# Three orders inside the queries' step: TensorE's output, VectorE's floor and finish, ScalarE's squares

## The chip, the core and the metric

The kernel runs on one core of one Trainium2 chip. The metric is the device time of one execution in microseconds (us). The engines work in parallel, each through its own instructions in order, and meet at semaphores: TensorE (PE, with its weight loads PEld), VectorE (DVE), ScalarE (ACT), GpSimd (POOL), and SyncE (SP), which here issues the transfers between HBM and SBUF.

## What is computed

Two layers with residuals on x of 16 x 256 x 64 x 64 (float32). Layer 0 is a group norm and a 3 x 3 convolution whose kernels are rotated per image by a small network. Layer 1 is a group norm and a focused linear attention with 8 heads and a 5 x 5 depthwise convolution of V.

```
x = x + conv(_gn(x))                      # layer 0: rotated 3x3 kernels, modulated
xt = _gn(x) as tokens                     # 4096 tokens of 256 channels
q = (relu(xt @ Wq.T + bq) + 1e-06) / scale
k = (relu(xt @ Wk.T + bk) + 1e-06) / scale
v = xt @ Wv.T + bv
q = q**3 / norm(q**3) * norm(q)           # the same for k
kv_state = einsum('bjc,bjd->bcd', k, v)
z = 1.0 / (einsum('bic,bc->bi', q, k.sum(axis=1)) + 1e-06)
out = einsum('bic,bcd->bid', q, kv_state) * z[..., None]
out = out + depthwise5x5(v)
x = x + out @ Wproj.T + bproj
```

## The kernel before, in words

Every engine has its own program, written by hand; the order of the code is the order of its instructions, and semaphore counters join them. The 16 images (batches b) go through three phases each: keys and values (16 half units of 256 tokens), the depthwise convolution, and the queries. Beside the queries of image b the engines do the layer 0 convolution of image b+2 and the input of the attention of image b+1. So batches 0 to 13 carry a convolution in the queries' phase, batch 14 only the next input, and batch 15 neither. Batches 0 to 12 are a hardware loop, the last three are unrolled.

The queries' phase is a software pipeline of steps (u, p), numbered n = 2u + p, of which each moves half a unit (256 tokens). In step n:

- TensorE (`step_q`, L1615) makes attention of half n-2, the output of half n-4, the transposes of O of half n-3, the projection of half n, the transposes of Q of half n-1, and a half plane of the convolution. In the step of u = 8 the keys of the next batch stand in the projection's place, in that of u = 9 its values.
- VectorE (`step_q`, L1066) does conv_out, cube of half n-1, denominators, inverses and quotients of half n-2, finish of half n-4 (it adds the output to the residual), result_stats, the cast of the attention's input (from u = 3), high (p = 1 only: the memsets of the borders of plane u+1 and its cast), ratio of half n-1, low_out of half n-3, and floor_max of half n, which waits for the projection.
- ScalarE (`step_q`, L1352) does planes (p = 1: the norm of plane u+1), sixths of half n-1 (behind cube), the norm of the attention's input, high_out of half n-3, shift (p = 0, behind result_stats), transposed_q (the copy QT of the transposes of Q, half n-1), norms (behind ratio), and squares of half n (behind floor_max).
- SyncE (`step`, L438) loads in p = 0 the residual of unit u-1 and stores x1. In p = 1 it loads the pixels, then waits until finish of both halves of unit u-2 is done (L375) and stores them, then loads the attention's input U (from u = 3), and then, when GpSimd has made the low half of plane u+1, the plane u+2 into PL (for u up to 5). All of it is one queue in order. PL is one buffer; ScalarE takes plane u+2 at the head of step (u+1, 1).

Attention of half n-2 in step n waits for the copy QT made in step n-1. Cube of half n waits for its squares. The output waits for low_out of its half.

Of the kernel before, what the change touches and what calls it, by code (L numbers as in the profile page):

```python
# [5 lines left out]
def conv_then_focused_attention(  # L6
# [58 lines left out]
    with ctx:  # L65
# [637 lines left out]
        def _(dve):  # L703
# [255 lines left out]
            def result_stats(c, k):  # L959
                g, q = divmod(k, 2)  # L960
                dve.wait_ge(x1_rdy, 2 * GROUPS * c + k + 1 + X1_CR)
                v.bn_stats(ST[:, 1, g, q, :], pixel_tile(c, g)[:, UNIT * q:UNIT * (q + 1)]).then_inc(s1_rdy, 1)
# [8 lines left out]
            def floor_max(n, p):  # L971
                dve.wait_ge(f_full, n + 1)
                fl = FL[:, :].unsqueeze(1).broadcast_to([P, 2, C])
                f = F[p][:, :].rearrange("p (t n) -> p t n", t=2)
                v.tensor_tensor(f, f, fl, ALU.max).then_inc(f_max, 1)  # L975
# [75 lines left out]
            def finish(b, u, p):  # L1051

                m = b * PAIRS + 2 * u + p
                dve.wait_ge(y_full, m + 1)
                dve.wait_ge(r_in[u % 2], Y_OUT * (b * NU // 2 + u // 2 + 1))
                r = R[:, u % 2, :, :, 2 * HD * p:2 * HD * (p + 1)].rearrange("p h m n -> p (h m) n")
                v.scalar_tensor_tensor(r, PP[:, :].rearrange("p (a n) -> p a n", n=2 * HD), out_fac, r,  # L1057
                                       ALU.mult, ALU.add).then_inc(y_rdy, 1)
# [8 lines left out]
            def step_q(b, u, p, live, nxt, keys, keys_end, conv):  # L1067
                n = b * 2 * PAIRS + PAIRS + 2 * u + p
                k = 2 * u + p - 1
                if conv and 0 <= k < 2 * GROUPS:  # L1070
                    conv_out(b + 2, k)
                if live(p - 1) or keys and p == 1 or keys_end and p == 0:
                    cube(n - 1, 1 - p)
                if live(p - 2):
                    denominators(b, u - 1, p)
                    inverses(b, u - 1, p)
                    quotients(b, u - 1, p)
                if live(p - 4):
                    finish(b, u - 2, p)
                if conv and 0 <= k < 2 * GROUPS:  # L1080
                    result_stats(b + 2, k)
                if nxt:
                    attn_input(b + 1, u - 3, p, False)
                if conv and p == 1 and u + 1 < GROUPS:
                    high(b + 2, u + 1)
                if live(p - 1):
                    ratio(n - 1, 1 - p, S6, S2)
                elif keys and p == 1:
                    ratio(n - 1, 1 - p, S2, S6)
                if live(p - 3):  # L1090
                    low_out(b, u - 2 + p, 1 - p)
                if live(p) or keys:
                    floor_max(n, p)
                if keys_end and p == 0:
                    scale_k(n - 2, 0)

# [148 lines left out]
        def _(act):  # L1245
# [43 lines left out]
            def squares(n, p):  # L1289
                act.wait_ge(f_max, n + 1 + MAX_CR)  # L1290
                act.wait_ge(f_cube, n + 1)
                act.wait_ge(f_six, 2 * n + 2)
                for t in range(2):
                    ts = slice(t * C, (t + 1) * C)
                    a.activation(K2[:, p, ts], F[p][:, ts], ACT.Square, scale=inv_a,  # L1295
                                 accum_out=S2[:, 2 * p + t:2 * p + t + 1]).then_inc(f_sq, 1)
# [57 lines left out]
            def step_q(b, u, p, live, nxt, keys, keys_end, conv):  # L1354
                n = b * 2 * PAIRS + PAIRS + 2 * u + p
                if conv and p == 1 and u + 1 < GROUPS:
                    planes(b + 2, u + 1)
                if live(p - 1) or keys and p == 1 or keys_end and p == 0:
                    sixths(n - 1, 1 - p)
                if nxt:  # L1360
                    attn_input(b + 1, u - 3, p)
                if live(p - 3):
                    high_out(b, u - 2 + p, 1 - p)
                if conv and p == 0 and 1 <= u <= GROUPS:
                    shift(b + 2, u - 1)
                if live(p - 1):
                    transposed_q(b, u - 1 + p, 1 - p)
                    norms(n - 1, 1 - p, den_eps)
                elif keys and p == 1:
                    norms(n - 1, 1 - p, inv_a2)  # L1370
                if live(p) or keys:
                    squares(n, p)

            def shift(c, g):

                act.wait_ge(s1_rdy, 2 * (GROUPS * c + g) + 2)
                tile = pixel_tile(c, g)
                a.activation(tile, tile, ACT.Identity, bias=BPC[:, g:g + 1]).then_inc(shifted, 1)
# [77 lines left out]
        def _(pe):  # L1456
# [143 lines left out]
            def output(b, u, p):  # L1600
                m = b * PAIRS + 2 * u + p
                pe.wait_ge(ol_rdy, m + 1 + OL_CR)
                pe.wait_ge(y_rdy, m + Y_CR)
                for h in range(HALVES):
                    k = 0
                    for kk in range(HALVES):
                        for wa, xa in PASSES:
                            ins = t_.matmul(PP[:, h * C:(h + 1) * C], WP[:, wa, kk, h * P:(h + 1) * P],  # L1608
                                            OT[:, xa, kk, 2 * P * p:2 * P * (p + 1)].rearrange(
                                                "p (y m x) -> p m y x", y=2, m=4),  # L1610
                                            start=(k == 0), stop=(k == 5))
                            k += 1
                ins.then_inc(y_full, 1)

            def step_q(b, u, p, live, conv, nxt):  # L1615

                if live(p - 2):
                    attention(b, u - 1, p)
                if live(p - 4):
                    output(b, u - 2, p)  # L1620
                if live(p - 3):
                    transpose_o(b, u - 2 + p, 1 - p)
                if live(p):
                    pe.wait_ge(f_cube, b * 2 * PAIRS + PAIRS + 2 * u + p + 1)
                    project(b, u, p, F, 0)
                elif nxt and u == NU:
                    keys(b + 1, 0, p)
                if live(p - 1):
                    transpose_q(b, u - 1 + p, 1 - p)
                if conv and u < GROUPS:  # L1630
                    convolve(b + 2, u, p)
                if nxt and u == NU + 1:
                    if p == 0:
                        pe.wait_ge(o_rdy, 2 * PAIRS * (b + 1) + O_CR)
                        carry(pe)
                    values(b + 1, 0, p)
# [147 lines left out]
```

## Time and profile before

| | us |
|---|---|
| median of 3 runs (3966.69 to 3974.39) | 3972.8 |
| the profiled execution | 3968.21 |
| its span | 3966.1 |
| TensorE busy | 3555.9 (90%) |
| VectorE busy | 2978.9 (75%) |
| ScalarE busy | 2704.6 (68%) |
| GpSimd busy | 1425.3 (36%) |
| L1057 finish, L975 floor_max: median of one | 0.742, 0.690 |
| L1346 copy of QT: median of one | 0.567 |

The middle of batch 5 is used as the sample. Its attention (L1587) starts at 1573.45 in step 2, 1579.11 in 3, 1585.18 in 4, 1592.46 in 5, 1599.74 in 6, 1607.02 in 7, 1614.31 in 8, 1621.59 in 9, 1628.87 in 10, 1636.37 in 11, 1643.76 in 12, 1651.40 in 13, 1658.79 in 14, 1666.45 in 15, 1673.84 in 16 and 1679.65 in 17. The other batches of the loop repeat this within some 0.03 us a step.

A share of busy time is an average over phases with different limits; what a change in the queries' step is worth is read from the steps themselves: who waits there, and for whom. A row of a timeline gives the start, the duration, the engine, the line, the operation, what it writes and reads, and in brackets the idle time before it with what ended it.

### The profile page before, as it was taken

What the parts mean: (1) busy time and instruction counts of PE and PEld (TensorE: products, weight loads), DVE (VectorE), ACT (ScalarE), POOL (GpSimd) and SP (SyncE); (2) the same over time, 40 slices, a digit from 0 to 9 for tenths busy, and PEclk for the clock granted to TensorE, in tenths of its full rate; (3) what the DMA queues carried; (4) which work ended last, traced back from release to release, by engine and by line L of the source; (5) the groups of instructions that cost most, each with busy time, mean ns of one, the idle gap of its engine ahead of it and who ended that gap; (6) DMA issues with size and microseconds to landing.
All of it is one profiled execution on the core that took longest, in us unless ns stands there. A gap on an engine that the chain in (4) does not pass through costs nothing.

```text
span 3966.1 us, 96093 instructions
## 1 busy us (share of the span) xinstructions
PE 3555.9 (90%) x27980; PEld 2859.5 (72%) x27980; DVE 2978.9 (75%) x8235; ACT 2704.6 (68%) x7348; POOL 1425.3 (36%) x1318
## 2 busy tenths in 40 slices
PE   0569989999999999999999998999999899999797
PEld 0138777777877777777777877777787777778686
DVE  6766877868778786877868687786868778585756
ACT  2247776776777677677766767776677767677675
POOL 4532442514334252433525243351424425140302
PEclk9989999999999999999999999999999999999999
DMA  4672634536354452635436263443636344260302
GB/s 156 202 236 65 173 98 143 161 90 186 109 155 116 131 173 82 184 112 149 130 111 192 71 184 113 138 141 108 179 91 178 99 145 132 79 181 22 102 17 75
DMA packets 560047, 516.42 MB, mean 130 GB/s; under 512 B 97600, under 2 KB 491968, under 8 KB 559552
## 3 DMA queue, kind: packets, MB, share of 16 engines
q1 hardware_dynamic: 555200, 508.99, 43.4%
q8 instruction: 220, 3.60, 0.4%
q14 instruction: 275, 2.25, 0.2%
q10 hardware_dynamic: 4352, 1.57, 0.2%
HBM read 351.06 MB, written 134.22 MB: 122 GB/s over the span
## 4 chain that ended last, share of the span: by engine, by line
PE 34%; DVE 29%; issue 17%; ACT 14%; DVEq 2%; DMA 1%; ACTq 1%; SPq 1%; POOL 1%; POOLq 0%
PE F L1557 7%; ACT K L1295 6%; PE VAB L1557 6%; PE F L1518 6%; PE VAB L1518 5%; PE T L1529 4%; DVE F L975 3%; DVE XR L1064 3%; ACT K L1301 3%; DVE XR L1057 3%; DVE XHL L969 3%; DVE K L981 2%; DVE XR L1046 2%; DVE RATIO L989 2%; PE PP L1608 2%
## 5 line engine op out<-in xcount | busy, mean ns | idle before, releaser
L1518 PE MATMUL F<-WQ,XHL 128*128 128x256 f16 x6144 | 819.3, 274 | 27.7 <-ACT V L1335 19.1
L650 POOL TENSOR_TENSOR XR<-XR,V 128x512 f32<-128x512 f32 x256 | 325.6, 1272 | 1042.9 <-DVE XR L1046 1042.9
L1518 PEld LDWEIGHTS F<-WQ,XHL 128*128 128x128 f16 (+1 forms) x6144 | 602.2, 99 | 106.8 <-issue 33.9
L1301 ACT ACTIVATE K<-K,SCAL 128x256 f32<-128x256 f32 x1024 | 512.4, 505 | 209.2 <-DVE K L981 208.2
L634 POOL TENSOR_TENSOR SL<-PL,SL 128x1122 f16<-128x1122 f32 x112 | 259.7, 2319 | 1065.2 <-DVE SL L947 1065.2
L1504 PE MATMUL SM<-SL,BD 128*128 128x512 f16 x2688 | 634.9, 385 | 0.0
L1295 ACT ACTIVATE K<-F,SCAL 128x256 f32<-128x256 f32 x1024 | 473.4, 469 | 232.0 <-DVE F L975 231.6
L975 DVE TENSOR_TENSOR F<-F,FL 128x512 f32<-128x512 f32 x512 | 354.1, 692 | 176.7 <-PE F L1520 175.4
L981 DVE TENSOR_TENSOR K<-K,F 128x512 f32<-128x512 f32 x512 | 349.3, 682 | 167.2 <-ACT K L1295 166.6
L1504 PEld LDWEIGHTS SM<-SL,BD 128*128 128x128 f16 x2688 | 261.0, 97 | 284.1
L1608 PE MATMUL PP<-XR,WP 128*128 128x256 f16 x3072 | 385.6, 276 | 67.8 <-DVE XR L1064 67.8
L1518 PE MATMUL VAB<-WQ,XHL 128*128 128x256 f16 x3072 | 414.6, 277 | 0.0
L1608 PEld LDWEIGHTS PP<-XR,WP 128*128 128x128 f16 x3072 | 297.9, 99 | 114.7 <-DVE XR L1064 76.9
L641 POOL TENSOR_TENSOR XHL<-U,XHL 128x512 f16<-128x512 f32 x256 | 297.9, 1170 | 208.8 <-DVE XHL L969 208.8
L1529 PE MATMUL T<-VT,K 128*128 128x129 f32 x2048 | 292.4, 287 | 71.7 <-DVE K L996 62.7
L1587 PEld LDWEIGHTS VAB<-KVS,VT 128*128 128x128 f32 x2048 | 261.6, 190 | 110.5 <-issue 46.7
L1518 PEld LDWEIGHTS VAB<-WQ,XHL 128*128 (+1 forms) x3072 | 305.5, 99 | 37.4
L1529 PEld LDWEIGHTS T<-VT,K 128*128 128x128 f32 x2048 | 258.0, 197 | 102.0 <-DVE K L996 94.3
L1587 PE MATMUL VAB<-KVS,VT 128*128 128x132 f32 x2048 | 282.4, 281 | 48.5 <-ACT VT L1346 44.1
L1557 PE MATMUL F<-V,TP 128*128 128x248 f16 (+1 forms) x2304 | 289.1, 282 | 0.0
L1520 PE MATMUL F<-BQ,ONES 128*128 128x256 f16 x1024 | 281.1, 275 | 0.0
L1307 ACT ACTIVATE NORM<-RATIO,SCAL 128x2 f32<-128x2 f32 x512 | 151.9, 297 | 175.8 <-DVE RATIO L989 175.1
(194 smaller groups left out, 6948.0 us busy)
## 6 DMA issues: line engine op xcount, KB each, us to landing
XR<-xr SPq DMA_DIRECT2D x132, 512.0 KB, 5.2
U<-x SPq DMA_DIRECT2D x256, 256.0 KB, 3.8
XR<-x SPq DMA_DIRECT2D x256, 256.0 KB, 4.1
out<-XR SPq DMA_DIRECT2D x256, 256.0 KB, 3.8
PL<-xp SPq DMA_DIRECT2D x112, 561.0 KB, 3.8
RX<-xr SPq DMA_DIRECT2D x118, 512.0 KB, 4.2
x<-RX SPq DMA_DIRECT2D x448, 128.0 KB, 2.1
BD<-RX SPq DMA_DIRECT2D x240, 96.0 KB, 2.2
```

What stands on the lines that cost most here:

```text
L641: g_.tensor_tensor(lo, U[:, u % 2, h].rearrange("p m y x -> p y m x"), hi, ALU.subtract).then_inc(l_rdy, 1)
L650: g_.tensor_tensor(o, o, fm, ALU.add).then_inc(o_rdy, 2)
L975: v.tensor_tensor(f, f, fl, ALU.max).then_inc(f_max, 1)
L981: v.tensor_tensor(K3[:, p, :], K2[:, p, :], F[p][:, :], ALU.mult).then_inc(f_cube, 1)
L1295: a.activation(K2[:, p, ts], F[p][:, ts], ACT.Square, scale=inv_a, accum_out=S2[:, 2 * p + t:2 * p + t + 1]).then_inc(f_sq, 1)
L1301: a.activation(K2[:, p, t * C:(t + 1) * C], K3[:, p, t * C:(t + 1) * C], ACT.Square, scale=inv_a, accum_out=S6[:, 2 * p + t:2 * p + t + 1] ...
L1504: ins = t_.matmul(conv_bank(c, q)[:, :], BD[:, j, HALVES * wa + h, sx, P * sy:P * (sy + 1)], half[:, xa, 16 * q + sy:16 * q + sy + 16, sx: ...
L1518: t_.matmul(o, XHL[:, xa, h, at], WQ[:, wa, h, c0:c0 + C], start=(k == 0), stop=False)
L1529: ins = t_.matmul(T[h][:, 0:P + 1], K3[:, p, t * C + h * P:t * C + (h + 1) * P], VT[:, p, t, h, 0:P + 1], start=False, stop=False)
L1557: ins = t_.matmul(bank[:, lo:hi], TP[:, c, d, ta, :], V[:, c, va, lo + sh:hi + sh], start=(k == 0), stop=(k == 8))
L1587: ins = t_.matmul(VA[t][:, h * KVC:(h + 1) * KVC], QT[:, p, h, t * P:(t + 1) * P], KVS[:, h, :], start=True, stop=True)
L1608: ins = t_.matmul(PP[:, h * C:(h + 1) * C], WP[:, wa, kk, h * P:(h + 1) * P], OT[:, xa, kk, 2 * P * p:2 * P * (p + 1)].rearrange("p (y m x ...
```

## The change

In the queries' step

- TensorE makes the output behind the projection (or the next batch's keys), no longer between attention and the transposes of O;
- VectorE does floor_max right behind result_stats, and finish last;
- ScalarE does the squares ahead of the copy QT and of norms, no longer behind them.

No instruction of the computation is added or removed, and SyncE's and GpSimd's programs are as they were.

```
@@ VectorE, step_q @@
-                if live(p - 4):
-                    finish(b, u - 2, p)
                 if conv and 0 <= k < 2 * GROUPS:
                     result_stats(b + 2, k)
+                if live(p) or keys:
+                    floor_max(n, p)
                 if nxt:
                     attn_input(b + 1, u - 3, p, False)
...
                 if live(p - 3):
                     low_out(b, u - 2 + p, 1 - p)
-                if live(p) or keys:
-                    floor_max(n, p)
+                if live(p - 4):
+                    finish(b, u - 2, p)
@@ ScalarE, step_q @@
+                if live(p) or keys:
+                    squares(n, p)
                 if live(p - 1):
                     transposed_q(b, u - 1 + p, 1 - p)
                     norms(n - 1, 1 - p, den_eps)
                 elif keys and p == 1:
                     norms(n - 1, 1 - p, inv_a2)
-                if live(p) or keys:
-                    squares(n, p)
@@ TensorE, step_q @@
                 if live(p - 2):
                     attention(b, u - 1, p)
-                if live(p - 4):
-                    output(b, u - 2, p)
                 if live(p - 3):
                     transpose_o(b, u - 2 + p, 1 - p)
                 if live(p):
...
                     keys(b + 1, 0, p)
+                if live(p - 4):
+                    output(b, u - 2, p)
```

VectorE, a step with the attention's input, p = 0 (L1046 quotients, L1057 finish, L962 result_stats, L975 floor_max, L969 cast of the input, L1064 low_out, L956 conv_out):

```order
 L1046 TENSOR_TENSOR XR<-VAB,Z 128x2x32x4 x2
-L1057 SCALAR_TENSOR_TENSOR XR<-PP,SCAL,XR 128x8x64
 L961 REGISTER_ALU
 L962 BN_STATS ST<-RX 128x6
+L972 REGISTER_ALU
+L975 TENSOR_TENSOR F<-F,FL 128x512
 L967 ISA
 L969 CAST XHL<-U 128x512
```

Floor_max went ahead of the cast, and finish left its place behind the quotients.

ScalarE, a step of p = 0 (L1378 shift, L1346 copy QT, L1307 norms, L1295 squares):

```order
 L1378 ACTIVATE RX<-RX,BPC 128x1024
-L1346 COPY VT<-T 128x512
-L1306 REGISTER_ALU
-L1307 ACTIVATE NORM<-RATIO,SCAL 128x2
-L1290 REGISTER_ALU
-L1292 REGISTER_ALU
-L1295 ACTIVATE K,S<-F,SCAL 128x256 x2
+L1290 REGISTER_ALU
+L1292 ISA
+L1295 ACTIVATE K,S<-F,SCAL 128x256 x2
+L1346 COPY VT<-T 128x512
+L1307 ACTIVATE NORM<-RATIO,SCAL 128x2
```

The squares moved between shift and the copy QT.

TensorE, a step from number 4 on (L1608 output, L1596 transposes of O, L1518 and L1520 projection):

```order
-L1608 MATMUL PP<-XR,WP 128x256 x12
-L1596 MATMUL T<-MATS,XR 128x128 x4
-L1518 MATMUL F<-WQ,XHL 128x256 x6
-L1520 MATMUL F<-BQ,ONES 128x256
-L1518 MATMUL F<-WQ,XHL 128x256 x6
-L1520 MATMUL F<-BQ,ONES 128x256
+L1596 MATMUL T<-MATS,XR 128x128 x4
+L1518 MATMUL F<-WQ,XHL 128x256 x6
+L1520 MATMUL F<-BQ,ONES 128x256
+L1518 MATMUL F<-WQ,XHL 128x256 x6
+L1520 MATMUL F<-BQ,ONES 128x256
+L1608 MATMUL PP<-XR,WP 128x256 x12
```

The output moved behind the projection, next to the transposes of Q.

## Rows read from the trace of the kernel before

**Rows 1.** Timeline of TensorE, batch 5, steps 11 to 13.

```profile
1636.37 1.16 PE L1587 MATMUL VAB<-KVS,VT 128*128 128x132 f32 x8
1637.37 1.47 PE L1608 MATMUL PP<-XR,WP 128*128 128x256 f16 x12
...
1639.12 0.82 PE L1518 MATMUL F<-WQ,XHL 128*128 128x256 f16 x6
...
1641.08 2.84 PE L1504 MATMUL SM<-SL,BD 128*128 128x512 f16 x12
1643.76 1.06 PE L1587 MATMUL VAB<-KVS,VT 128*128 128x132 f32 x8
...
1651.40 1.16 PE L1587 MATMUL VAB<-KVS,VT 128*128 128x132 f32 x8
```

**Rows 2.** Timeline of ScalarE, the same stretch: shift, QT, planes, sixths, input, squares.

```profile
1634.62 1.15 ACT L1378 ACTIVATE RX<-RX,BPC 128x1024 f32<-128x1024 f32 x1
1635.68 0.56 ACT L1346 COPY VT<-T 128x512 f32<-128x512 f32 x1
...
1637.79 1.32 ACT L1281 ACTIVATE PL<-PL,PR 128x1122 f32<-128x1122 f32 x1
1639.00 0.50 ACT L1301 ACTIVATE K<-K,SCAL 128x256 f32<-128x256 f32 x1
...
1639.98 0.81 ACT L1286 ACTIVATE U<-U,PR 128x512 f32<-128x512 f32 x1
...
1645.37 0.47 ACT L1295 ACTIVATE K<-F,SCAL 128x256 f32<-128x256 f32 x1 [1.05 <-DVE F L975]
```

**Rows 3.** Timeline of VectorE, the same: input's cast, plane's cast, low_out, floor, cube.

```profile
1641.05 0.56 DVE L969 CAST XHL<-U 128x512 f16<-128x512 f32 x1
...
1642.52 1.03 DVE L947 CAST SL<-PL 128x1122 f16<-128x1122 f32 x1
...
1643.91 0.74 DVE L1064 SCALAR_TENSOR_TENSOR XR<-T,SCAL,XR 128x512 f16<-128x512 f32 x1
1644.57 0.69 DVE L975 TENSOR_TENSOR F<-F,FL 128x512 f32<-128x512 f32 x1
...
1646.51 0.69 DVE L981 TENSOR_TENSOR K<-K,F 128x512 f32<-128x512 f32 x1 [0.61 <-ACT K L1295]
```

**Rows 4.** Timeline of batch 14: two starts of attention, a cast, a cube.

```profile
3702.83 0.96 DVE L969 CAST XHL<-U 128x512 f16<-128x512 f32 x1
...
3703.82 1.17 PE L1587 MATMUL VAB<-KVS,VT 128*128 128x132 f32 x8 [1.36 <-ACT VT L1346]
...
3706.58 0.69 DVE L981 TENSOR_TENSOR K<-K,F 128x512 f32<-128x512 f32 x1 [1.09 <-ACT K L1295]
...
3710.19 1.17 PE L1587 MATMUL VAB<-KVS,VT 128*128 128x132 f32 x8 [1.36 <-ACT VT L1346]
```

**Rows 5.** Timeline of TensorE, batch 15: an attention, and the last output.

```profile
3886.76 1.17 PE L1587 MATMUL VAB<-KVS,VT 128*128 128x132 f32 x8 [0.68 <-ACT VT L1346]
...
3959.99 1.48 PE L1608 MATMUL PP<-XR,WP 128*128 128x256 f16 x12 [1.57 <-DVE XR L1064]
```

**Rows 6.** Timeline of TensorE, batch 5: its last two outputs.

```profile
1686.33 1.48 PE L1608 MATMUL PP<-XR,WP 128*128 128x256 f16 x12 [2.24 <-DVE XR L1064]
...
1692.07 1.48 PE L1608 MATMUL PP<-XR,WP 128*128 128x256 f16 x12 [2.29 <-DVE XR L1064]
```

**Rows 7.** Timeline of SyncE's queue, batch 5: store, U load, PL load.

```profile
1641.99 1.44 SPq L378 DMA_DIRECT2D out<-XR  x2
1643.77 1.66 SPq L348 DMA_DIRECT2D U<-x  x2
1646.28 0.38 SPq L328 DMA_DIRECT2D PL<-xp  x1
```

**Rows 8.** DMA issues, time to landing: the PL load of 1646.28, and that of 1600.91.

```profile
PL<-xp SPq DMA_DIRECT2D x1, 561.0 KB, 5.1
...
PL<-xp SPq DMA_DIRECT2D x1, 561.0 KB, 3.7
```

More of the change, by code:

```diff
@@ L1077, in step_q @@
                     quotients(b, u - 1, p)
-                if live(p - 4):
-                    finish(b, u - 2, p)
                 if conv and 0 <= k < 2 * GROUPS:
                     result_stats(b + 2, k)
+                if live(p) or keys:
+                    floor_max(n, p)
                 if nxt:
@@ L1091, in step_q @@
                     low_out(b, u - 2 + p, 1 - p)
-                if live(p) or keys:
-                    floor_max(n, p)
+                if live(p - 4):
+                    finish(b, u - 2, p)
                 if keys_end and p == 0:
@@ L1365, in step_q @@
                     shift(b + 2, u - 1)
+                if live(p) or keys:
+                    squares(n, p)
                 if live(p - 1):
@@ L1370, in step_q @@
                     norms(n - 1, 1 - p, inv_a2)
-                if live(p) or keys:
-                    squares(n, p)
             def shift(c, g):
@@ L1618, in step_q @@
                     attention(b, u - 1, p)
-                if live(p - 4):
-                    output(b, u - 2, p)
                 if live(p - 3):
@@ L1627, in step_q @@
                     keys(b + 1, 0, p)
+                if live(p - 4):
+                    output(b, u - 2, p)
                 if live(p - 1):
```

## The prediction, made before the changed kernel ran

> **What bounds the kernel now.** First the busy shares on the first page of the profile: TensorE is busy for 90% of the span, VectorE 75%, ScalarE 68%, so a step counts only where TensorE stands still in it, or is made to. So the second view is TensorE's timeline of the queries' steps, with the starts of attention as a ruler (numbers of steps: 2u+p). Three kinds of batches differ.
>
> Batches 0 to 13 carry a convolution in steps 0 to 15. In one late step attention takes 1.00 us, output with O's transposes 1.75, projection with Q's transposes 1.96, the convolution 2.68: 7.39, of which 0.1 belongs to the wait before it; the next step ends 7.64 later [rows 1]. Without waits a step is 7.28, as steps 4 to 9 are. From step 4 to step 16 attention moves from 1585.18 to 1673.84: 88.66, against 12 x 7.28 = 87.36. So 1.3 us per batch are waits, all in the last six steps. Their source is on VectorE: floor at 1644.57, the squares on ScalarE 0.80 later, and cube not before 1646.51, after an idle 0.61 [rows 2, 3]. Two late steps take 15.03 [rows 1]; less two such waits VectorE's own work is 13.8 of the 14.56 that TensorE needs, and with them it is over.
>
> Batch 14 has no convolution: its steps take 6.37, VectorE idles 1.09 in each before cube, and TensorE 1.36 before attention [rows 4]. Batch 15 has less VectorE work: 5.55 a step, which is TensorE's own 4.7 (1.00 + 1.75 + 1.96 [rows 1]) plus the time until the copy of QT, for which it idles 0.68 [rows 5].
>
> Third, the end of each batch. There output waits 2.24 and then 2.29 us for low_out [rows 6]; at the very end 1.57 [rows 5].
>
> **The change, part by part.** Nothing is added; the orders of TensorE, VectorE and ScalarE change, SyncE's does not.
>
> Floor ahead, finish last. Floor(n) moves ahead of cast, ratio and low_out, right after the sums. The squares then run under these and cube(n) no longer waits. This takes the 0.61 and 1.09 off VectorE. In batches 0 to 13 TensorE gets at most the 1.3 us. In batch 14 VectorE's load falls from 6.37 to 5.3, below the 5.55 that TensorE and the QT copy need in batch 15: 0.82 less for each of 9 steps, 0.3 for the one before, 7.7 in all.
>
> Output behind the projection. This brings floor's input 1.3 us earlier, else floor would wait in its new place. For TensorE the sum stays. At a batch's end O's last transposes no longer stand behind an output that waits. I walked it with the rows' durations: seen from attention of step 16 the last output starts 16.7 later instead of 18.23 (1692.07 [rows 6] less 1673.84), a gain of 1.55. In batch 14 I get 1.5, because the copies of V then wait for the U load of unit 7; at the end of batch 15, 1.9.
>
> Squares ahead of QT's copy. They put 0.92 us (two of 0.47 [rows 2]) in front of a copy that TensorE's next attention needs. Where the convolution stands between, it has 2.68 us of cover, but in steps of p=0 shift stands in front too: shift 1.06, copy to attention 0.69 [rows 1, 2], and squares between. The cover is gone at step 2, where shift is late: attention of step 3 comes 0.35 later. At step 16, without a convolution, it comes 0.8 later (inside the 1.55). In steps 2 to 4 of batches 14 and 15 neither output nor convolution is there, and projection, floor, squares, copy become one chain: attention is later by 0.95, 0.95 and 0.8 to 1.2, so 2.7 in batch 14 and 3.2 in batch 15.
>
> The queue behind finish. This speaks against the change. SyncE is in order: it waits for finish of step n, issues the two stores, then the U load, then the plane load PL, which ScalarE needs at the head of step n+2 (n odd). Today finish comes early and the store is held by a pixel load; PL is held by GpSimd's low half (the U load is out at 1645.43, PL starts 1646.28 [rows 7]). Now finish is VectorE's last work in the step that also has the plane's memsets and cast, and PL has one buffer. The cycle, from the start of planes on ScalarE: sixths +1.21, attention's input +0.98 [rows 2], its cast +0.90, the plane's cast +1.47, low_out +1.39, finish +0.66 [rows 3] (finish is taken to start where floor did), its end and the store +0.84, U +1.78 [rows 7], PL +1.97 (the U issues 1.66, and a gap of 0.3), then its landing L and 0.1 for the wait: 11.3 + L, less 0.2 where the U issue is shorter. L was 3.7 for a PL load without U in front and 5.1 and more with it [rows 8]. In between, L = 4.1, is what I take, since the pixel load, just ahead of the store in those late cases, is then some four us ahead and done. So a pair takes 15.2 to 15.3, and three pairs per batch are behind a U load (planes 5, 6, 7: steps 9 to 15). Against 3 x 14.56 that is +2.2, with 0.05 for step 8. Ends: with L = 3.7, +1.0; with 5.1, +5.2 per batch.
>
> The port. The cast of the attention's input takes 0.56 [rows 3], and in batch 14, beside a GpSimd addition, 0.96 [rows 4]. In its new place, by my walk, it starts some 0.3 before GpSimd's addition ends. If it ran at half speed beside it, that would cost 0.15 a step, and the sum has room for that in VectorE's idle time. The Trainium skill (SBUF — State Buffer, section SBUF: two separate sides) says that of the two engines the one that starts first holds their shared port pair for its whole instruction, and the other is blocked. By it the cast would be held for those 0.3, and the sum would be the same, except at steps where VectorE is late, which would be later by 0.15 more.
>
> **Sum**, on the profiled execution (span 3966.1, time 3968.2). Batches 0 to 12: +0.35 + 2.25 - 1.3 - 1.55 = -0.25 each, -3.2. Batch 13, whose code is unrolled, has only 0.5 of waits to give back: 0.35 + 2.0 - 0.5 - 1.55 = +0.3. Batch 14: +2.7 - 7.7 - 1.5 = -6.5. Batch 15: +3.2 - 1.9 = +1.3. In all -8.1. The profiled execution lies 4.6 under the median 3972.8, so I forecast 3972.8 - 8 = 3965.
>
> **Rivals.**
> - The plane load does not bind. If L is 3.4 or less, or the chain has slack that I missed, pairs take 14.6: -2.4 per batch against the sum's -0.25. Times 14 this is -30 more: 3935. For it: PL loads of 3.7 exist [rows 8]. Against it: U and store go just ahead. The Trainium skill (DMA: Bandwidth & Descriptors, section Anatomy of one DMA — SWDGE (gpsimd) path) fits one transfer by 2.0 us plus its bytes over 436 GB/s, for another way of issuing. For 561 KB this is an estimate of 3.3 us, and by it this rival would hold; the trace disagrees, with 3.7 and 5.1 [rows 8].
> - Slower: the queue behind finish binds fully. One mechanism, one place: PL lands late and holds ScalarE's planes, with everything behind them. Each us of L costs 3 us per batch, 42 in all. It decides from L = 4.3 (total zero). With L = 5.1, as today's late ones, +42 on the forecast: 4007; with L = 6, 4045. For it: U directly before PL, as in today's late cases. Against it: the pixel load is gone from in front.
> - No change: the change does what it says, but TensorE has its own 7.28 nearly everywhere, and what the ends give the heads and copies take. Mine is the sum of small terms of both signs, so 3972 is near.
> - The squares' place costs more than priced. In a p=0 step cube, sixths, attention's input, O's high copy, shift, squares and QT's copy follow each other: attention of the next step is 6.33 after VectorE's first instruction of the step. That fits into 7.28 if VectorE starts less than 0.95 late, and each 0.2 more costs 5 steps x 14 x 0.2 = 14 us: 3980.
>
> **How the numbers follow.** A measurement of this kernel tells about 0.2%, 8 us, from no change. I give my forecast 0.38, the free plane load 0.20, the bound queue 0.20, no change 0.12, the copies 0.10. The forecast lies on the border of 0.2%, so its chance is halved over faster and same, with little over slower. Faster 0.45, same 0.28, slower 0.27. The range is to leave out 1 in 5: it reaches 3930 (free plane load with a little more) and 4010 (L = 5.1).
>
> **What would show it.** Right: in batches 0 to 12, cube without idle time before it; steps 4 to 9 at 7.28; pairs 9-11, 11-13, 13-15 of 15.0 to 15.5, with ScalarE's planes released by the DMA of PL; attention of step 3 later by 0.35; idle before the last outputs 1.2 instead of 2.3; batch 14 at 5.55 a step after a head 2.7 longer; batch 15 with att(1) and att(2) later and the same 5.55. Wrong: pairs of 14.6 (then the queue was overpriced), pairs over 16, or ScalarE's copy releasing attention in the middle steps.

## The result: 1.4% slower, and the profile after

| | before | after |
|---|---|---|
| median (3 runs; 4 runs) | 3972.8 | 4026.45 (4024.36 to 4031.19) |
| after over before, 95% interval | | 1.0138 [1.0125, 1.0151] |
| profiled execution, its span | 3968.21, 3966.1 | 4024.36, 4022.3 |
| TensorE busy | 3555.9 (90%) | 3576.2 (89%) |
| VectorE busy | 2978.9 (75%) | 2946.3 (73%) |

The forecast was 3965, in a range of 3930 to 4010. The time is 61 us above the forecast and 16 above the range's upper end. A fourth run of the kernel before, beside the changed one, took 3967.30.

The spans of the profiled executions added up by stage, from TensorE's timeline (us; a loop batch is the mean of batches 1 to 12; "attention 2" is the one of step 2):

| stage | loop batch before, after | batch 13 | batch 14 | batch 15 |
|---|---|---|---|---|
| keys and values | 65.74, 66.57 | 65.70, 63.98 | 61.07, 61.07 | 61.37, 61.99 |
| to attention 2 | 44.48, 44.52 | 42.43, 42.52 | 39.93, 40.83 | 39.30, 40.96 |
| attention 2 to 17 | 106.22, 111.46 | 105.01, 110.07 | 88.62, 87.67 | 80.54, 82.59 |
| attention 17 to the next batch | 17.62, 15.82 | 14.81, 13.47 | 16.01, 13.47 | |

So the loss stands in one place: 5.2 us per batch between attention 2 and 17. In batch 5 attention now starts, from step 9 on, 7.98, 8.28, 7.38, 8.01, 8.36 and 8.27 us apart, where it was 7.28 to 7.67 before; steps 4 to 9 stay at 7.28. Over the loop, the three pairs from step 9 to step 15 take 16.34 on average, against the 15.25 of the forecast and TensorE's 14.56.

Who is waited for there is on ScalarE. Timeline of ScalarE after, batch 5, steps 13 and 15: planes, and between them sixths, squares and the copy of QT.

```profile
1660.73 1.32 ACT L1281 ACTIVATE PL<-PL,PR 128x1122 f32<-128x1122 f32 x1 [1.96 <-DMA PL<-xp]
...
1669.18 0.51 ACT L1301 ACTIVATE K<-K,SCAL 128x256 f32<-128x256 f32 x1 [2.27 <-DVE K L981]
...
1672.49 0.46 ACT L1295 ACTIVATE K<-F,SCAL 128x256 f32<-128x256 f32 x1
...
1673.39 0.57 ACT L1346 COPY VT<-T 128x512 f32<-128x512 f32 x1
...
1677.37 1.32 ACT L1281 ACTIVATE PL<-PL,PR 128x1122 f32<-128x1122 f32 x1 [3.21 <-DMA PL<-xp]
```

The planes of [rows 2] had no wait; these stand still for 1.96 and 3.21 us until the transfer PL has landed, and the whole kernel has 48 such waits, 126.1 us. All 42 loads of planes 5, 6 and 7 are among them. Before the change there were none. The loads of PL in the trace after, whole kernel: who waits for them, and the time from issue to landing.

```profile
who waited for it (us, times):
  ACT PL L1281: 126.1, 48
...
DMA to landing us min/median/max: 3.4/3.9/6.2
```

Why PL is late can be read off VectorE and SyncE. Timeline of VectorE after, between the two planes: the attention's input waits behind ScalarE, and finish closes the step.

```profile
1663.77 0.43 DVE L969 CAST XHL<-U 128x512 f16<-128x512 f32 x1 [1.21 <-ACT U L1286]
...
1665.11 1.03 DVE L947 CAST SL<-PL 128x1122 f16<-128x1122 f32 x1
...
1666.49 0.74 DVE L1064 SCALAR_TENSOR_TENSOR XR<-T,SCAL,XR 128x512 f16<-128x512 f32 x1
1667.15 0.74 DVE L1057 SCALAR_TENSOR_TENSOR XR<-PP,SCAL,XR 128x512 f32<-128x512 f32 x1
1667.81 0.74 DVE L956 SCALAR_TENSOR_TENSOR RX<-SM,MODC,RX 128x512 f32<-128x512 f32 x1
1668.47 0.68 DVE L981 TENSOR_TENSOR K<-K,F 128x512 f32<-128x512 f32 x1
```

SyncE's queue after, the same stretch: pixel load, stores, U load, PL load (an x2 line has two transfers, and its time is that of issuing them).

```profile
1664.59 0.37 SPq L333 DMA_DIRECT2D RX<-xr  x1
1668.04 1.44 SPq L378 DMA_DIRECT2D out<-XR  x2
1669.82 1.44 SPq L348 DMA_DIRECT2D U<-x  x2
1671.58 0.38 SPq L328 DMA_DIRECT2D PL<-xp  x1
```

DMA issues after, time to landing: this PL load.

```profile
PL<-xp SPq DMA_DIRECT2D x1, 561.0 KB, 5.8
```

This is the cycle that the prediction describes. Planes at 1660.73, finish ends at 1667.89, store +7.31 after planes, U +1.78, PL +1.76, landing 5.8, the next planes at 1677.37: 16.64. In [rows 7] the U load was out 2.5 us before PL, which waited for GpSimd's low half; now the low half is done 0.75 after finish, and nobody waits for it. The cycle sets the pairs one by one: in batches 1 to 12 the landings differ from 4.25 to 6.03 us in planes 6 and 7, and each of the 24 pairs of attention 11 to 13 and 13 to 15 takes what the planes are apart, within 0.02 us (15.14 at the shortest landing, 16.92 at the longest).

What the change was to give is there. Cube, with an idle time of 0.61 and 1.09 in [rows 3, 4], starts without any in the last VectorE row above.

### The profile page after: what moved, and what is told of

It reads as the page before. It is cut to its first block, busy times and chain, and to the rows that moved or that the text cites. A ratio compares the mean times of both kernels' runs of the same rounds, so it can differ in the third digit from the quotient of the medians.

```text
span 4022.3 us, 95872 instructions
## 1 busy us (share of the span) xinstructions
PE 3576.2 (89%) x27980; PEld 2859.2 (71%) x27980; DVE 2946.3 (73%) x8235; ACT 2678.4 (67%) x7348; POOL 1424.6 (35%) x1318
## 4 chain that ended last, share of the span: by engine, by line
PE 53%; DVE 15%; issue 13%; ACT 13%; DMA 3%; SPq 2%; DVEq 1%; ACTq 1%; POOL 0%; POOLq 0%
PE F L1518 10%; PE SM L1504 7%; PE F L1557 7%; PE VAB L1557 6%; PE VAB L1518 5%; PE T L1529 4%; PE VAB L1587 4%; ACT K L1301 4%; ACT K L1295 3%; PE PP L1608 3%; DVE K L981 2%; ACT U L1286 2%; PE F L1520 2%; PE T L1596 2%; DVE F L975 2%
## 5 line engine op out<-in xcount | busy, mean ns | idle before, releaser
L1518 PE MATMUL F<-WQ,XHL 128*128 128x256 f16 x6144 | 825.4, 276 | 27.0 <-ACT V L1335 19.0
L1518 PEld LDWEIGHTS F<-WQ,XHL 128*128 128x128 f16 (+1 forms) x6144 | 605.1, 99 | 108.4 <-issue 33.3
L1295 ACT ACTIVATE K<-F,SCAL 128x256 f32<-128x256 f32 x1024 | 470.4, 465 | 119.2 <-DVE F L975 117.9
L975 DVE TENSOR_TENSOR F<-F,FL 128x512 f32<-128x512 f32 x512 | 353.9, 691 | 212.3 <-PE F L1520 206.6
L1518 PE MATMUL VAB<-WQ,XHL 128*128 128x256 f16 x3072 | 407.8, 274 | 0.0
L1608 PE MATMUL PP<-XR,WP 128*128 128x256 f16 x3072 | 377.1, 272 | 23.1 <-DVE XR L1057 22.6
L1608 PEld LDWEIGHTS PP<-XR,WP 128*128 128x128 f16 x3072 | 298.4, 98 | 64.4 <-DVE XR L1064 26.6
L1518 PEld LDWEIGHTS VAB<-WQ,XHL 128*128 (+1 forms) x3072 | 301.9, 98 | 33.8
L1520 PE MATMUL F<-BQ,ONES 128*128 128x256 f16 x1024 | 282.4, 276 | 0.0
L1557 PE MATMUL VAB<-V,TP 128*128 128x248 f16 (+1 forms) x2304 | 270.1, 270 | 0.0
```

The lines of the kernel that those rows point to most:

```text
L1518: t_.matmul(o, XHL[:, xa, h, at], WQ[:, wa, h, c0:c0 + C], start=(k == 0), stop=False)
L1520: ins = t_.matmul(o, ONES[:, :], BQ[:, c0:c0 + C], start=False, stop=True)
L1557: ins = t_.matmul(bank[:, lo:hi], TP[:, c, d, ta, :], V[:, c, va, lo + sh:hi + sh], start=(k == 0), stop=(k == 8))
```

## Experiments: which piece makes the late steps

All kernels but e5, e6 and e7 start from the changed one; e7 is the kernel before with one line moved. The landing, here and in the table further down, is the mean over the loads of planes 5, 6 and 7 of batches 1 to 13.

**e1: the plane load ahead of the stores.**

```
@@ SyncE, step, p = 1 @@
+                    if s2 and u + 2 < GROUPS:
+                        planes_after(b + 2, u + 2, GROUPS * (b + 2) + u + 2)
                     if 2 <= u < NU + 2:
                         store(b, u - 2, 0)
                         store(b, u - 2, 1)
                     if s1 and 3 <= u <= NU:
                         next_unit(b + 1, u - 1)
-                    if s2 and u + 2 < GROUPS:
-                        planes_after(b + 2, u + 2, GROUPS * (b + 2) + u + 2)
```

> The changed kernel with one thing moved in SyncE's program: in a step of p = 1 the plane load PL is issued ahead of the two stores and of the U load, no longer behind them. Theory (the plane load behind finish sets the pairs of late steps): PL goes out when GpSimd's low half is made, about 7.9 us after the start of planes instead of 10.9, and lands in about 4; the cycle is 12, below the 14.56 of TensorE, so pairs 9-11, 11-13, 13-15 fall from 15.4 to 16.9 to 14.6. The excess over 7.28 a step is about 5.4 per batch, 75 in all: about 3951. Rival (squares ahead of the copy of QT, or VectorE's new order, are what makes the late steps of 8.3 long): SyncE's order is irrelevant, pairs stay above 15.7 and the time within 10 us of 4026.

Measured: 3951.07 (five runs, 3936 to 3956), ratio to before 0.9941 [0.9921, 0.9962]. Every step from 4 to 16 is 7.28 in batches 1 to 13, with four exceptions of up to 0.13, and attention 2 to 17 takes 106.05 in the loop. Of the waits for PL 14.4 us are left. So SyncE's order alone takes 75 us from the changed kernel, and the rival falls.

**e4: only the U load behind the plane load.**

```
@@ SyncE, step, p = 1 @@
                         store(b, u - 2, 1)
-                    if s1 and 3 <= u <= NU:
-                        next_unit(b + 1, u - 1)
                     if s2 and u + 2 < GROUPS:
                         planes_after(b + 2, u + 2, GROUPS * (b + 2) + u + 2)
+                    if s1 and 3 <= u <= NU:
+                        next_unit(b + 1, u - 1)
```

> The changed kernel with the U load issued behind the plane load, stores still ahead of both. Theory: the cycle loses the 1.8 us between U and PL, and the landing, with no U load directly in front, falls from 5.5 to 4.1 to 5.0; 7.3 + 1.8 + 4.1 to 5.0 = 13.2 to 14.1, below 14.56: pairs of 14.6, about 3952. If the landing stays at 5.5, pairs are 14.6 to 15.0: 3960. Rival (squares, VectorE): 4026.

Measured: 3947.5, ratio to before 0.995 [0.9933, 0.9968]; attention 2 to 17 takes 106.05. SyncE's queue of e4, batch 5: stores, PL, U.

```profile
1643.94 1.44 SPq L378 DMA_DIRECT2D out<-XR  x2
1645.72 0.38 SPq L328 DMA_DIRECT2D PL<-xp  x1
1646.42 1.45 SPq L348 DMA_DIRECT2D U<-x  x2
```

ScalarE of e4: QT, norms, and planes right behind them, for this load.

```profile
1649.29 0.57 ACT L1346 COPY VT<-T 128x512 f32<-128x512 f32 x1
...
1649.76 0.30 ACT L1307 ACTIVATE NORM<-RATIO,SCAL 128x2 f32<-128x2 f32 x1
1649.95 1.32 ACT L1281 ACTIVATE PL<-PL,PR 128x1122 f32<-128x1122 f32 x1
```

Waits for PL in e4, whole kernel: 9.8 us of the 126.1 are left.

```profile
  ACT PL L1281: 9.8, 22
```

The landing falls from 5.5 to 4.5 on average. Both parts of the gain, 1.8 of place in the queue and 1.0 of landing, were in the expectation. The stores behind finish could stay where they are: without the U load between them and PL the cycle fits. Batch 13 is an exception in the landing: there, in the same order, it takes 5.1 to 5.7, and the cause of that stays open.

**e2: finish directly behind floor, SyncE as changed.**

```
@@ VectorE, step_q @@
                 if live(p) or keys:
                     floor_max(n, p)
+                if live(p - 4):
+                    finish(b, u - 2, p)
                 if nxt:
                     attn_input(b + 1, u - 3, p, False)
...
                     low_out(b, u - 2 + p, 1 - p)
-                if live(p - 4):
-                    finish(b, u - 2, p)
```

> The changed kernel with finish directly behind floor on VectorE, ahead of the input's cast, instead of last; SyncE as before. Theory: finish ends about 3.5 us earlier in a step of p = 1, store and U load go out while GpSimd still makes its low half, and PL leaves with the low half, 8 us after the start of planes; with a landing of 5 that is 13, below 14.56: pairs of 14.6 to 14.9, about 3955. Rival (squares or VectorE's load): 4026 or, since finish now waits for the output in the middle of VectorE's step, above it.

Measured: 3983.84, ratio to before 1.0035 [1.0023, 1.0048]: of the waits for PL only 6.2 us are left in the whole kernel, much as expected, but the pairs are 15.05, not 14.6 to 14.9. VectorE of e2, one step of p = 1 in batch 5:

```profile
1649.76 0.75 DVE L956 SCALAR_TENSOR_TENSOR RX<-SM,MODC,RX 128x512 f32<-128x512 f32 x1 [0.99 <-PE SM L1504]
...
1653.87 0.75 DVE L1057 SCALAR_TENSOR_TENSOR XR<-PP,SCAL,XR 128x512 f32<-128x512 f32 x1 [0.40 <-PE PP L1608]
...
1657.25 0.74 DVE L1064 SCALAR_TENSOR_TENSOR XR<-T,SCAL,XR 128x512 f16<-128x512 f32 x1
```

TensorE of e2, the next step: the transposes of O wait for that low_out.

```profile
1658.13 0.63 PE L1596 MATMUL T<-MATS,XR 128*128 128x128 f32 x4 [0.30 <-DVE XR L1064]
```

The step of VectorE begins when a half plane of the convolution is ready (1649.76) and its low_out ends 8.2 us later, 0.3 too late for TensorE. Finish with its wait of 0.40 now stands ahead of low_out. So finish last is worth something, by what it lets ahead, and a late finish alone is not what hurts: e1 and e4 have it and no late steps.

**e3: the squares back behind QT and norms.**

```
@@ ScalarE, step_q @@
-                if live(p) or keys:
-                    squares(n, p)
                 if live(p - 1):
                     transposed_q(b, u - 1 + p, 1 - p)
...
+                if live(p) or keys:
+                    squares(n, p)
```

> The changed kernel with the squares back behind the copy of QT and norms; output, floor and finish as changed. Theory: the squares are not in the cycle of the plane load, so pairs of late steps stay at 15.4 to 16.9; only the heads and step 17 give back: step 3 by 0.35 and step 17 by 0.75 in 14 batches, batch 14's head by 6 to 7, batch 15's by 2.3: about 4026 - 24 = 4002. Rival (the squares' place is the cause of the late steps): pairs near 15.0 as before the change, the time near 3965.

Measured: 4005.47 (three runs at 4004 to 4007, one at 3987), ratio to before 1.0075 [1.0046, 1.0103], against 4002 expected. The late pairs stay (attention 2 to 17 takes 110.4 in the loop, the landing 5.5), step 17 is 5.66 instead of 6.56, and batch 14 takes 80.59 from attention 2 to 17 instead of 87.67. So the squares' place is not the cause of the late steps, only of the heads. ScalarE of e3, batch 5, planes of step 13:

```profile
1656.55 1.33 ACT L1281 ACTIVATE PL<-PL,PR 128x1122 f32<-128x1122 f32 x1 [2.95 <-DMA PL<-xp]
```

## Experiments: the pieces alone, and a control

**e5: the output behind the projection alone** (the kernel before, with TensorE's hunk of the change).

> The kernel before with TensorE's output behind the projection alone. Theory: finish, in its old place behind the quotients, waits for the output, which ends some 4.4 us after attention starts instead of 2.5, so VectorE idles some 2 us in every step from number 4 on; its load of 13.8 per pair becomes 17 or so, less the 0.6 per step it idles before cube now; pairs near 15 to 16 in all batches: 3990 to 4050. Rival (the output's place is neutral for VectorE): 3968.

Measured: 4085.69, ratio 1.0288 [1.027, 1.0306], above the expected range. In the late steps attention is 7.38 and 8.6 to 8.7 us apart by turns, and nobody waits for PL. VectorE of e5, a step of p = 1: both waits in a row, the one before cube and the new one before finish.

```profile
1700.90 0.69 DVE L981 TENSOR_TENSOR K<-K,F 128x512 f32<-128x512 f32 x1 [0.61 <-ACT K L1295]
...
1703.84 0.75 DVE L1057 SCALAR_TENSOR_TENSOR XR<-PP,SCAL,XR 128x512 f32<-128x512 f32 x1 [1.09 <-PE PP L1608]
```

**e6: floor ahead and finish last alone** (the kernel before, with VectorE's hunk).

> The kernel before with VectorE's floor behind result_stats and finish last, but the output in its old place ahead of the projection, and the squares in theirs. Theory: floor's input is ready 1.3 us later than in the changed kernel, so floor waits 1 us or more in each step, and the plane load still stands behind a late finish: pairs of late steps above 15.5, 4000 to 4050. Rival (the plane load is late only with the squares moved): near 3968.

Measured: 4080.45, ratio 1.0275 [1.0257, 1.0293]. The expectation named the mechanism and sized it too small: floor waits 0.60 to 1.00 for the projection in most late steps, and the plane load is late as well (42 waits, 112.1 us).

```profile
1698.99 0.70 DVE L975 TENSOR_TENSOR F<-F,FL 128x512 f32<-128x512 f32 x1 [1.00 <-PE F L1520]
...
1700.59 0.43 DVE L969 CAST XHL<-U 128x512 f16<-128x512 f32 x1 [0.89 <-ACT U L1286]
```

So the output's move and VectorE's need each other: each alone costs 2.8% to 2.9%, both together 0.75% (that is e3), and with the squares' move 1.4%. The squares' move alone on the kernel before was not run.

**e7: the U load behind the plane load, in the kernel before** (SyncE's edit of e4 alone).

> The kernel before with one thing moved: SyncE issues the U load behind the plane load. It tells whether the 20 us that this order gives over the kernel before come from it alone. Theory: no; in the kernel before the late steps wait for VectorE's floor, squares and cube, and PL leaves with GpSimd's low half; late steps keep 7.4 and 7.65, 3966 to 3970. Rival (the U load in front of PL costs the kernel before its 1.3 us per batch too): late steps 7.28, 14 x 1.3 = 18 less, 3950.

Measured: 3969.11, ratio 0.9995 [0.9987, 1.0004]. The late steps are 7.38 and 7.66 as before, though the landing falls from 4.95 to 3.8. So the gain of e4 does not come from SyncE's order alone: in the kernel before PL did not bind, and the three moves pay only once it is out of the way.

## Experiments: the heads of the last batches, and a better version

The head of batch 14 grew far more than forecast. Attention 2 to 5 takes 6.69 + 7.11 + 7.22 = 21.02 us, where it took 4.08 + 4.65 + 5.55 = 14.28. TensorE after, these steps:

```profile
3722.51 1.82 PE L1587 MATMUL VAB<-KVS,VT 128*128 128x132 f32 x8 [1.84 <-ACT VT L1346]
3724.13 1.49 PE L1518 MATMUL F<-WQ,XHL 128*128 128x256 f16 x6
...
3729.20 1.68 PE L1587 MATMUL VAB<-KVS,VT 128*128 128x132 f32 x8 [1.88 <-ACT VT L1346]
...
3736.31 1.96 PE L1587 MATMUL VAB<-KVS,VT 128*128 128x132 f32 x8 [1.88 <-ACT VT L1346]
```

Busy time of the engines in the three steps from attention 2 to 5, and in a part of the first one, after; PEclk is the clock granted to TensorE as a share of 2.4 GHz.

```profile
core 0: us, PE busy (x) PEld busy (x) DVE busy (x) ACT busy (x) POOL busy (x), PEclk, DMA share, GB/s
3722.51:3729.20 6.69, 4.80 (x27) 3.85 (x27) 2.98 (x10) 2.79 (x11) 1.28 (x1) 0.74 0.00 0
3729.20:3736.31 7.11, 5.23 (x30) 4.43 (x30) 3.61 (x11) 3.46 (x12) 1.26 (x1) 0.76 0.00 0
3736.31:3743.53 7.22, 6.55 (x42) 5.73 (x42) 3.73 (x12) 3.57 (x12) 1.27 (x1) 0.76 0.01 2
...
3723.00:3726.00 3.00, 3.00 (x16) 2.43 (x15) 1.18 (x4) 0.83 (x4) 0.21 (x1) 0.50 0.00 0
```

The waits for the copy of QT grew from 0.94 to 1.84, which is the 0.9 a step of the forecast. But behind such a wait attention takes 1.7 to 2.0 us instead of 1.17, and six matmuls of the projection 1.49 instead of 0.82: the granted clock is 0.74 to 0.76 of 2.4 GHz over the three steps, and 0.50 behind the first wait, which is the lower level of 1.2 GHz. To tell the wait from the clock, e9 fills the wait with work of no use.

**e9: matmuls in the waits.**

```
@@ TensorE, step_q @@
                 if live(p - 1):
                     transpose_q(b, u - 1 + p, 1 - p)
+                if not conv and (u, p) in ((0, 1), (1, 0), (1, 1)):
+                    pe.wait_ge(x1_rdy, 2 * GROUPS * B + X1_CR)
+                    for k in range(12):
+                        t_.matmul(SM[:, 0:C], WP[:, 0, 0, 0:P], WP[:, 0, 0, :], start=True, stop=True)
```

> The changed kernel with 12 more matmuls of 128x256 on TensorE, whose product nobody reads, behind the transposes of Q in steps 1, 2 and 3 of batches 14 and 15, where TensorE otherwise waits 1.84 to 1.88 us for the copy of QT. They take 1.3 us of each wait and put no step off. Theory (the waits of 1.9 us let TensorE's clock fall to its lower level, and that costs 4.0 of the 6.7 us by which the head of batch 14 grew): with less idle time the granted clock stays at 1.0 there, attention takes 1.17 again instead of 1.7 to 2.0, and attention 2 to 5 of batch 14 takes 17 us instead of 21.0. Rival (the waits are the whole cost, the clock follows from something else): 21.0 as before, or more by the fillers' own time.

TensorE of e9, the same steps: the filler (L1633), the wait that is left, attention.

```profile
3727.24 1.47 PE L1633 MATMUL SM<-WP 128*128 128x256 f16 x12
3729.25 1.17 PE L1587 MATMUL VAB<-KVS,VT 128*128 128x132 f32 x8 [0.54 <-ACT VT L1346]
...
3732.22 1.47 PE L1633 MATMUL SM<-WP 128*128 128x256 f16 x12
3734.26 1.17 PE L1587 MATMUL VAB<-KVS,VT 128*128 128x132 f32 x8 [0.57 <-ACT VT L1346]
```

Its clock, the same columns as above:

```profile
3729.00:3732.00 3.00, 2.75 (x25) 2.59 (x26) 1.64 (x6) 1.48 (x6) 0.13 (x1) 1.00 0.03 5
3732.00:3735.00 3.00, 2.43 (x22) 2.02 (x21) 1.77 (x5) 2.20 (x9) 1.14 (x1) 1.00 0.00 0
```

Measured: attention 2 to 5 of batch 14 takes 5.01 + 5.45 + 5.56 = 16.02, 5.0 less than after (1.0 more than expected), with every clock at 1.00. Doing more work made the stretch shorter. With attention 2 later by 0.95 (40.88 against 39.93), the head costs 16.02 - 14.28 + 0.95 = 2.7 us: the forecast's number, to which the clock had added 5.0. The Trainium skill (TensorE: Matmul & The Clock Gate, section Part 1: The HAM clock gate) says that the array's clock is set by how busy it has been recently, and this pair of traces agrees. The time of e9 is 4023.78, ratio 1.0143 [1.0124, 1.0162]; 5 us of 4026 are too few to show there.

The waits alone don't fix what the clock does. In batch 15 after, three waits of nearly the same lengths (1.84, 1.66 and 1.88) have a clock of 0.74 in the first step and 1.00 in the other two, and the steps take 6.46, 5.45 and 5.56 (5.01, 5.45 and 5.55 in e9). In e1, whose TensorE program is that of after, the same steps take 7.44, 5.45 and 7.22 with a clock of 0.58, 1.00 and 0.76. And the kernel before has a clock of 0.69 in the first of them, behind a wait of 0.93: 5.47 us, where e7, with the same TensorE program, has 1.00 and 4.08. So both batch 15 figures hold some 1.4 us of low clock. What decides between them was not found.

**e8: U load behind the plane load, squares ahead of QT only where a convolution covers them.** SyncE's edit of e4, and:

```
@@ ScalarE, step_q @@
-                if live(p) or keys:
+                first = conv and u < GROUPS
+                if first and (live(p) or keys):
                     squares(n, p)
                 if live(p - 1):
...
+                if not first and (live(p) or keys):
+                    squares(n, p)
```

> The changed kernel with two things: the U load behind the plane load, and the squares ahead of the copy of QT only in steps with a convolution (u under 8 in batches 0 to 13), elsewhere behind it as before. Theory: late steps 7.28 as with the U load behind; step 17 back to 5.7 or so (0.9 less in 14 batches, 12 in all); batch 14's head 7 less, batch 15's 2 less: 3947 - 21 = 3927. Rival (these gains are given back behind the last attention, where the last outputs wait for low_out): only the heads, 3938.

Measured: 3938.08, ratio to before 0.9919 [0.9906, 0.9932]: the rival's 3938. Batch 14's attention 2 to 17 takes 80.60 (87.67 in e4) and batch 15's 80.39 (82.53). Step 17 is 5.66 again, but from attention 17 to the next batch the loop takes 16.6 instead of 15.4 of e4: what that step gives (0.9) is taken back behind it.

**e10 and e11.** e10 keeps the squares ahead in steps 16 and 17 too (first = conv); e11 is the kernel of e8 again, on the same chip.

> The changed kernel with the U load behind the plane load, and the squares ahead of the copy of QT in all steps of batches 0 to 13 (step 16 and 17 too), behind it in batches 14 and 15. Theory: in the profiles of e4 and e8, attention 16 to the next batch's start took 7.0 + 15.0 = 22.0 and 5.7 + 17.0 = 22.7 us in the loop, so the squares' old place in step 16 gained nothing; here 22.0 stays and batches 14 and 15 give back 9.2: 3938 or up to 8 less than e8 beside it. Rival (the 0.7 is noise of the loop's edge): the same as e8 within 4.

> The kernel of e8 again, unchanged, beside e10 on the same chip: 3938.

Measured: 3937.96 (0.9921 [0.9903, 0.9938]) and 3941.19 (0.9923 [0.9905, 0.9942]). The same within the intervals. From attention 16 to the next batch the loop (mean of batches 1 to 12) takes 22.2 in e10, 22.2 in e8 and 22.3 in e11, so by the traces the place in steps 16 and 17 is worth 0.2 us a batch at most. The 22.7 of e8 in the expectation was read 0.5 too high: it is 5.66 + 16.56. The three orders of the change, with the U load behind the plane load and the squares confined to the convolution's batches, are 0.8% faster than the kernel before.

| | median | ratio to before | attention 2 to 17, loop | landing |
|---|---|---|---|---|
| before | 3972.8 | | 106.2 | 4.95 |
| after | 4026.45 | 1.0138 | 111.5 | 5.5 |
| e1 PL ahead of stores | 3951.07 | 0.9941 | 106.05 | 4.8 |
| e4 U behind PL | 3947.5 | 0.995 | 106.05 | 4.5 |
| e2 finish behind floor | 3983.84 | 1.0035 | 108.0 | 4.2 |
| e3 squares back | 4005.47 | 1.0075 | 110.4 | 5.5 |
| e5 output alone | 4085.69 | 1.0288 | 113.9 | 4.2 |
| e6 floor, finish alone | 4080.45 | 1.0275 | 112.0 | 5.4 |
| e7 before, U behind PL | 3969.11 | 0.9995 | 106.2 | 3.8 |
| e8 best | 3938.08 | 0.9919 | 105.1 | 4.4 |
| e9 filler | 4023.78 | 1.0143 | 111.5 | 5.5 |
| e10 squares ahead in all of 0 to 13 | 3937.96 | 0.9921 | 106.0 | 4.5 |
| e11 best again | 3941.19 | 0.9923 | 105.1 | 4.4 |

## Why the prediction was wrong

**The step that failed: the landing L of the plane load.** The mechanism was right and one term of it was too small. The prediction wrote the cycle down (finish, stores, U load, PL load, planes), made it the one thing that speaks against the change, and found 11.1 + L. Measured is 7.31 + 1.79 + 1.77 = 10.9 + L. For L it took 4.1, between the 3.7 and 5.1 of [rows 8], on the ground that the pixel load would be gone from in front. It is gone from the place next to it (1664.59, 3.45 ahead of the store), and L is 5.5 on average, 4.3 to 6.2. The 5.1 of [rows 8] was the row with a U load directly in front, the very situation of the change, and the pixel load was a distinction that no row had tested. The other two late loads of the same batch before took 6.1 and 4.8, and the mean over batches 1 to 13 is 4.95: put into the prediction's sum for the 4.1, this alone gives 3965 + 0.85 x 42 = 4001. The rest came with the change. U's issue began 2.5 us ahead of PL in the loop before, while PL waited for GpSimd, and 1.8 us ahead after; over these runs the landing is the longer, the nearer the U load stands (last section).

With L = 5.5 the prediction's own line for the slower rival (4007 at 5.1, 42 more per us) gives 4024, against 4026 measured. That this is so close is luck: the line puts 59 us on the queue, the pairs measure about 45 of the 64 by which the profiled execution is over the sum, and the rest comes from other terms of the table below and from another phase. The chance of 0.20 was too low. The upper end of the range was put at L = 5.1, a typical late row and not the end of the late rows.

The fixed part of the cycle came out 0.2 under the forecast, of which 0.13 is the cast of the input: in a step of p = 1 it takes 0.43 after, and the forecast had the 0.56 of [rows 3]. One of its sums is misread: from the attention's input to its cast the rows give 1.07 (1639.98 to 1641.05), where it has 0.90.

**The rest of the sum, term by term.**

| term, us per batch | forecast | measured |
|---|---|---|
| late waits before cube | -1.3 | gone |
| late pairs above 14.56, three | +2.2 | +5.4 |
| step 3 | +0.35 | +0.34 |
| step 17 (inside attention 16 to the last output) | +0.8 | +0.75 |
| attention 16 to the last output (batch 5) | -1.55 | -1.13 |
| batch 14, steps of 6.37 to 5.55 | -7.7 | -7.7 |
| batch 14, head | +2.7 | +7.6 |
| batch 14, end | -1.5 | -2.5 |
| batch 15, head | +3.2 | +3.85 |
| batch 15, attention 16 to the last output | -1.9 | -1.2 |

The pairs miss by 3.2, which in 14 batches is about 45 of the 64 us by which the two profiled executions miss the forecast's -8.1 (4024.36 less 3968.21 is +56.1). The head of batch 14 misses by 5, all of it the clock (e9). At a batch's end the walk overlooked a wait: the last output stands behind finish of the output before it, which is now VectorE's last work. TensorE after, batch 5:

```profile
1710.11 0.63 PE L1596 MATMUL T<-MATS,XR 128*128 128x128 f32 x4 [1.00 <-DVE XR L1064]
1710.77 1.47 PE L1608 MATMUL PP<-XR,WP 128*128 128x256 f16 x12
...
1715.21 1.47 PE L1608 MATMUL PP<-XR,WP 128*128 128x256 f16 x12 [1.44 <-DVE XR L1057]
```

The idle times of 2.24 and 2.29 of [rows 6] went to 1.00 and 1.44, and of the gain only half, 1.05 per batch, reaches the start of the next batch in the loop. The phase of keys and values is longer by 0.8 per loop batch, 10 us in all, and nothing in the change reaches it. The other kernels show 65.5 to 66.9 in the same phase, and two executions of one kernel, e8 and e11, differ by 0.3, so it may be variation between executions; that stays open.

**The other rivals.** The free plane load did not come (an L of 3.4 was seen in none of the planes 5 to 7), but e1 and e4 produce it by other means: 3951 and 3947, where the rival gave 3935. Of the difference the heads of batches 14 and 15 are 9 (e8 gives them back and has 3938). The 3.3 us that the prediction worked out from the Trainium skill (DMA: Bandwidth & Descriptors, section Anatomy of one DMA — SWDGE (gpsimd) path) for a transfer of this size is the best case here, in planes 0 to 4, which average 3.7 to 4.0; behind the U load it is 5.5, and the measurement decides. The copies were not the bound: attention's waits in the middle steps go back to planes, and with PL in time (e4) the steps of both kinds are 7.28 with the squares in their new place.

**The port.** The cast of the input takes 0.43 in a step of p = 1 after, and 0.64 in a step of p = 0, where it starts before a GpSimd addition ends. VectorE and GpSimd after: batch 5, and an earlier pair that overlaps for longer.

```profile
1656.02 0.64 DVE L969 CAST XHL<-U 128x512 f16<-128x512 f32 x1
...
766.90 1.33 DVE L969 CAST XHL<-U 128x512 f16<-128x512 f32 x1 [0.28 <-ACT U L1286]
```

```profile
1655.09 1.28 POOL L650 TENSOR_TENSOR XR<-XR,V 128x512 f32<-128x512 f32 x1 [1.86 <-DVE XR L1046]
...
766.80 1.15 POOL L641 TENSOR_TENSOR XHL<-U,XHL 128x512 f16<-128x512 f32 x1 [0.93 <-DVE XHL L969]
```

The additions end at 1656.37 and 767.95, the casts at 1656.66 and 768.23: 0.28 to 0.29 later both times. So it is in all 121 casts of this trace, and in all 203 of the one before, that start while a GpSimd instruction runs that has more than 0.25 us to go: they end 0.28 to 0.29 after it. The 23 casts that started ahead of GpSimd's instruction took 0.41 to 0.43, like the 123 beside none. At half speed, as the prediction's sum had it, none could take more than twice 0.43, and this one takes 1.33. So that reading was wrong, and the Trainium skill's rule of a port that one engine holds and the other is blocked from (SBUF — State Buffer, section SBUF: two separate sides) describes this case, with GpSimd's spans as the trace has them. The cost is 0.2 in a step of p = 0, where the sum had 0.15, and it is not what moved the time.

## What to carry to other kernels

When a step of an engine moves to the end of its loop, look at what is queued behind the transfer that waits for it: here a store waited for finish, and behind the store stood a load of a single buffer that closed a cycle of 16.4 us around a loop of 14.56. Price such a cycle with the landings that the trace shows in that same queue position, the slowest for the end of the range, and if the sum hangs on it, reorder the queue in the same edit; one line of SyncE's order turned 1.4% slower into 0.5% faster. Moves that hand work from one engine to the next should be priced together: alone, two of these pieces cost 2.8% to 2.9% each, and together 0.75%.

## What the runs showed of the hardware that was not expected

- A wait that grows from 0.94 to 1.84 us can cost more than its length. In batch 14, with three such waits in a row, TensorE's granted clock was 0.74 to 0.76 over three steps (5.0 us lost); with 1.47 us of unused matmuls in each wait it was 1.00. Nearly the same waits in batch 15 lowered it in one step of three.
- The same 561 KB load lands the later, the nearer a U load stands in front of it (planes 5 to 7, batches 1 to 12). With U's issue 1.8 us ahead it takes 5.3 to 5.5 on average (after, e3, e6, e9), with 2.5 us 5.0 (before), with 3.0 us 4.2 (e2, e5). With U behind it, it takes 4.3 to 4.4 with the stores 1.8 us ahead (e4, e8, e10, e11) and 3.8 with the stores 4.4 us ahead (e7). This is no full account: in e1, ahead of them all and 2.1 us behind the pixel load, it takes 4.8, and in batch 13 of e4, e8, e10 and e11, in the same order, 5.4 to 5.7. How the 16 engines share the transfers was not taken apart.
- A VectorE cast that starts while a GpSimd addition runs ends 0.28 to 0.29 us after it, whatever the overlap (324 casts in two traces): up to 1.4 us instead of 0.43.
